# Perceiver block on one Trainium2 core: who turns the context of the first cross attention, and how it travels

## The chip, the cores and the metric

The kernel runs on one core of a Trainium2 chip. Its engines are TensorE (PE; PEld is its weight load), VectorE (DVE), ScalarE (ACT), GpSimd (POOL) and SyncE (SP), which here only issues DMA transfers. The metric is the device time of one execution in microseconds, as the median of several runs. Lower is better.

## The reference, cut to what matters

128 batches, each of 32 latents by 128 features (`x`) and 257 context rows by 128 features. Six residual stages follow each other; the change lies in the first, a cross attention with 16 heads of 64:

```python
xn = layer_norm(ctx_1024, g1, b1)                    # 257 rows a batch
ln_lat = layer_norm(layernorm(x), g2, b2)            # 32 rows a batch
q = ln_lat @ Wq
k, v = split(concatenate([xn, ln_lat], axis=1) @ Wkv)
weight = einsum('bhld,bhnd->bhln', q * scale, k * scale)   # 289 keys
weight = softmax(where(full_mask, weight, -max))
x = x + einsum('bhln,bhnd->bhld', weight, v) @ Wout
...
x = x + recurrence(x); x = x + ffn(x)
x = x + cross_attention_16_heads_of_8(x, ctx_1024)
x = x + self_attention(x); x = x + mixture_of_experts(x)
```

## The kernel before

The stages run one after another. The first cross attention is the function `xattn0`, and it is one software pipeline over the 128 batches: each engine runs `step(g, j)` for the step `s = 8g + j`, and within a step works on batches that are some steps ahead. `run_steps` writes the first 8 steps and those ahead of them out, loops over groups of 8, and writes the last ones out. Semaphores with growing counts order the engines; nothing else does, so the written order of each engine's `step` is the order of the work. The second cross attention (`xattn1`) uses `run_steps` too.

Weights are folded so that keys and values need no projection of their own. Scores of a batch are products of a query matrix (`qT`) and the transposed, normalised context (`xnT`, 256 columns of context, 32 of latents, one of the context's last row). Queries, and `xnT` too, are held as a rounded upper half (HI) and the rest (LO), and the score is a sum of three products. Four batches make a tile; once in four steps (`b == 0`) TensorE projects the finished tile (16 products, which the trace shows as `a_ctx<-U,a_oT` since they share a PSUM bank with the turned context).

One batch `n` passes as follows, by the step in which each thing happens before the change:

- `n-8`: SP loads its raw context (`load_raw`); `n-7`: VectorE takes mean and variance, GpSimd the reciprocal root; `n-6`: VectorE makes `z`, GpSimd multiplies by `g1` and adds `b1` (L671, L673), giving `xn`.
- `n-5`: TensorE turns the two halves of `xn` into the bank `a_ctx` (L884), between the two value products of another batch. ScalarE copies the bank to HI of `xnT` (L815), VectorE subtracts to get LO (L763).
- `n-3`: TensorE scores in four groups (L830), VectorE masks and takes the smallest (L705, "masks"), ScalarE takes the exponential with its sum (L778), VectorE the reciprocal (L755).
- `n-2`: ScalarE normalises the probabilities (L786, four instructions). VectorE transposes them in blocks of 32 x 32 into `blocks` (L716, 1024 columns; L718, 256 columns). `spread_prob` on SP then sends each of four quarters of `blocks` to `probT` (L625, four transfers of 192 KB), which completes the transposition. It waits for the blocks and for the value products that last read this one of the two `probT` buffers (`out_ready`).
- `n`: TensorE multiplies values and probabilities (L840, L847); ScalarE copies the result out in the next step (L796).

In every step TensorE also makes a quarter of the queries of a tile ahead (L856), ScalarE and VectorE split them (L811, L750). The order of VectorE's step is: masks, transposes, statistics, `z`, aggregation, query, reciprocal, (addition to `x`), LO of the context. That of ScalarE: result of the last batch, normalisation, four exponentials, query, HI of the context.

## Time and profile before

| | |
|---|---|
| median of 3 runs | 2055.96 us (2054.47 to 2059.8) |
| the profiled execution | 2053.8 us, of which its span 2051.7 us |
| granted TensorE clock, mean | 0.914 |
| PE busy | 1718.3 us, 84% |
| DVE busy | 1594.6 us, 78% |
| ACT busy | 1504.4 us, 73% |
| POOL busy | 908.9 us, 44% |
| DMA, all queues | 259.54 MB, mean 127 GB/s |

The span runs from the first to the last instruction of one profiled execution, and the time of that execution is a little longer. "Busy" is the time in which an engine's data path works; an engine's busy intervals can overlap with its next instruction's, so a group's busy sum can be less than count times duration. The clock is given as a share of full speed. Sizes such as 128x256 are partitions by elements.

### The profile page before, as it was taken

The numbers are of one execution on the slowest core, as the hardware profiler recorded it, in microseconds if no ns is written. First come the engines' busy times: TensorE is split into PE (matmuls) and PEld (weight loads), VectorE is DVE, ScalarE is ACT, GpSimd is POOL, SyncE is SP. The second block draws the span as 40 slices with busy tenths as digits, with TensorE's granted clock in tenths as the row PEclk, the third lists the DMA queues.
The fourth block names the chain that finished last, engine by engine and source line by source line (L and its number), as shares of the span: only waits on it lengthen the run. The fifth ranks groups of instructions, "written<-read, shape, count | busy, mean of one in ns | idle before, by whom it ended". The sixth has DMA issues, their size and how long they took to land. (4 is left out here: it accounts for less than half of the span.)

```text
span 2051.7 us, 51500 instructions
## 1 busy us (share of the span) xinstructions
PE 1718.3 (84%) x13455; PEld 1392.9 (68%) x13455; DVE 1594.6 (78%) x4998; ACT 1504.4 (73%) x4156; POOL 908.9 (44%) x1339
## 2 busy tenths in 40 slices
PE   3599999999999999971710679999999799749997
PEld 3489999999999999941500356666667566427775
DVE  4798888888888888837788669999999588636664
ACT  3488888888888888854765479999999588545553
POOL 1544444444444444304156034444444377335554
PEclk8599999999999999995755799999999799879998
DMA  4277676777777777610000059999999300103322
GB/s 139 85 167 165 160 160 157 161 163 162 159 162 163 159 160 164 151 42 0 0 0 0 2 147 250 252 250 251 249 249 248 73 1 0 32 13 102 91 87 82
DMA packets 196234, 259.54 MB, mean 127 GB/s; under 512 B 25136, under 2 KB 141328, under 8 KB 196032
## 3 DMA queue, kind: packets, MB, share of 16 engines
q1 hardware_dynamic: 194678, 256.53, 50.0%
q10 hardware_dynamic: 1194, 1.58, 0.3%
q0 software_dynamic: 288, 0.56, 0.1%
q8 instruction: 33, 0.54, 0.1%
q14 instruction: 41, 0.34, 0.0%
HBM read 86.09 MB, written 4.72 MB: 44 GB/s over the span
## 5 line engine op out<-in xcount | busy, mean ns | idle before, releaser
L778 ACT ACTIVATE a_prob<-a_neg,a_nmax 128x289 f32<-128x289 f32 x512 | 266.6, 525 | 1.4 <-DVE a_nmax L705 1.1
L840 PE MATMUL a_out<-a_probT,a_xn 128*128 128x256 f32 x1024 | 263.0, 380 | 5.0 <-DMA a_probT<-a_blocks 4.2
L1710 ACT ACTIVATE b_prob<-b_neg,b_nmax 128x257 f32<-128x257 f32 x512 | 260.6, 515 | 6.9 <-DVE b_nmax L1661 6.8
L671 POOL TENSOR_TENSOR a_xn<-a_z,g 128x256 f32<-128x256 f32 x128 | 93.8, 733 | 384.6 <-DVE a_z L739 384.6
L830 PE MATMUL a_score<-a_xnT,a_qT 128*128 128x290 f32 x1536 | 252.9, 314 | 2.5 <-DVE a_qT L750 2.5
L705 DVE CUSTOM_DVE_ANT_0 a_neg<-a_score,a_bias 128x289 f32<-128x289 f32 x512 | 211.6, 458 | 41.2 <-PE a_score L830 36.8
L786 ACT ACTIVATE a_prob<-a_prob,a_rinv 128x289 f32<-128x289 f32 x512 | 231.3, 527 | 1.8 <-DVE a_rinv L755 1.7
L830 PEld LDWEIGHTS a_score<-a_xnT,a_qT 128*128 128x128 f32 x1536 | 222.3, 190 | 9.6 <-issue 3.3
L1661 DVE CUSTOM_DVE_ANT_0 b_neg<-b_score,b_bias 128x257 f32<-128x257 f32 x512 | 188.6, 419 | 30.5 <-PE b_score L1801 15.3
L840 PEld LDWEIGHTS a_out<-a_probT,a_xn 128*128 128x128 f32 x1024 | 175.2, 191 | 19.8 <-DMA a_probT<-a_blocks 5.3
L716 DVE STREAM_TRANSPOSE a_blocks<-a_prob 128x1024 f32<-128x1024 f32 x128 | 159.4, 1245 | 24.0 <-ACT a_prob L786 17.7
L2417 POOL TENSOR_TENSOR m_hidden<-m_full,m_hidden 128x512 fp32r<-128x512 f32 (+1 forms) x88 | 113.7, 1292 | 106.6 <-ACT m_hidden L2398 106.6
L1672 DVE STREAM_TRANSPOSE b_blocks<-b_prob 128x1024 f32<-128x1024 f32 x128 | 156.3, 1221 | 0.2
L856 PE MATMUL a_q<-latT,A 128*128 (+1 forms) x1024 | 140.0, 281 | 12.4 <-DVE a_qT L750 10.1
L856 PEld LDWEIGHTS a_q<-latT,A 128*128 128x128 f32 x1024 | 131.0, 197 | 14.2 <-DVE a_qT L750 11.6
L847 PE MATMUL a_out<-a_probT,a_tail 128*128 128x256 f32 x512 | 131.4, 379 | 0.0
L796 ACT ACTIVATE a_oT<-a_out 128x512 f32<-128x512 f32 x128 | 76.6, 598 | 72.2 <-PE a_out L847 72.2
L872 PE MATMUL a_ctx<-U,a_oT 128*128 128x128 f32 x1024 | 119.7, 275 | 0.7 <-ACT a_oT L796 0.7
L2393 ACT ACTIVATE m_silu<-m_g 128x512 f32<-128x512 f32 (+1 forms) x88 | 52.7, 598 | 89.7 <-PE m_g L2047 89.7
L872 PEld LDWEIGHTS a_ctx<-U,a_oT 128*128 128x128 f32 x1024 | 116.9, 192 | 1.1 <-ACT a_oT L796 1.1
L1634 POOL TENSOR_TENSOR b_last_part<-b_v_rows,b_prob 128x128 f32<-128x128 f32 x128 | 52.0, 407 | 138.9 <-ACT b_prob L1710 134.1
L847 PEld LDWEIGHTS a_out<-a_probT,a_tail 128*128 128x128 f32 x512 | 97.3, 190 | 13.2
(478 smaller groups left out, 4567.9 us busy)
## 6 DMA issues: line engine op xcount, KB each, us to landing
a_probT<-a_blocks SPq DMA_DIRECT2D x512, 192.0 KB, 3.6
b_probT<-b_blocks SPq DMA_DIRECT2D x256, 256.0 KB, 4.6
a_raw<-in_ctx SPq DMA_DIRECT2D x128, 128.0 KB, 2.9
b_raw<-in_ctx SPq DMA_DIRECT2D x64, 256.0 KB, 4.7
m_wide<-expert_weights SPq DMA_DIRECT2D x128, 128.0 KB, 2.9
a_kept<-keep SPq DMA_DIRECT2D x32, 257.0 KB, 3.4
b_kept<-keep SPq DMA_DIRECT2D x32, 257.0 KB, 4.8
b_v_rows<-ctx_tail_values SPq DMA_DIRECT2D x32, 256.0 KB, 4.7
```

Of the source, the lines that this page charges most:

```text
L705: nc.vector.tensor_tensor_reduce(out=neg[:, grp, :], in0=score_ps[grp][:, 0:KEYS0], in1=bias[:, n, :], scale=-DH0 ** -0.5, scalar=3.4e38, ...
L716: nc.vector.transpose(blocks[:, n, :, 0:2].rearrange("p r t g l -> p g r t l"), prob[:, n, :, 0:2 * P].rearrange("p g (r t c) -> p g r t c ...
L778: nc.scalar.activation(prob[:, par, grp, 0:KEYS0], neg[:, grp, :], ACT.Exp, bias=nmax[:, par, grp:grp + 1], scale=-1.0, accum_out=rsum[:, ...
L786: last = nc.scalar.activation(part, part, ACT.Copy, scale=rinv[:, j % 2, grp:grp + 1])
L830: last = nc.tensor.matmul(score_ps[grp][:, 0:even(KEYS0)], qT[:, a, un, bn, 4 * grp:4 * grp + 4, :], xnT[:, c, n, :], start=(p == 0), stop ...
L840: nc.tensor.matmul(out_ps[:, half, 0:2 * P], xn[:, j, kt, :], probT[:, u, 2 * half:2 * half + 2, kt, :], start=(kt == 0), stop=False)
L847: last = nc.tensor.matmul(out_ps[:, half, 0:2 * P], tail[:, j, :], probT[:, j % 2, 2 * half:2 * half + 2, 2, :], start=False, stop=True)
L856: last = nc.tensor.matmul(q_ps[:, h * P:(h + 1) * P], k.A[:, 4 * hg + h, :], k.latT[:, ds((t + ahead) * P, P)], start=True, stop=True)
L872: last = nc.tensor.matmul(proj_ps, oT[:, slot, :], k.U[:, slot % GROUPS * HG + slot // GROUPS, :], start=(slot == 0), stop=(slot == H - 1))
L1661: nc.vector.tensor_tensor_reduce(out=neg[:, par, grp, :], in0=score_ps[grp][:, 0:N_CTX], in1=bias[:, n, :], scale=-DH1 ** -0.5, scalar=3.4 ...
L1672: nc.vector.transpose(blocks[:, n, :, j % 2].rearrange("p r t g l -> p g r t l"), prob[:, j % 4, :, 0:2 * P].rearrange("p g (r t c) -> p g ...
L1710: nc.scalar.activation(prob[:, (j + 5) % 4, grp, :], neg[:, par, grp, :], ACT.Exp, bias=nmax[:, par, grp:grp + 1], scale=-1.0, accum_out=r ...
```

## The change

- The context is no longer turned on TensorE. VectorE transposes `xn` in 32 x 32 blocks, in `turn_blocks`, into 64 more columns of `blocks`, six batches ahead; `spread_prob` carries them to `probT` together with the probabilities of the batch two ahead. Rows of both buffers grow from 384 to 448 elements, and each of the four transfers with them.
- HI of `xnT` is copied by ScalarE from the landed `probT` four batches ahead, behind the copy of the last result; LO is now subtracted by GpSimd, from SBUF. `spread_prob` waits also for that (`xnT_ready`), and VectorE's transposes of a buffer wait for its last landing.
- The bank `a_ctx` goes; the projection has its own, `a_proj`. `z` is written into `xn` directly.
- Raw context is loaded ten batches ahead instead of eight, its statistics taken eight ahead, `z` seven.
- VectorE's order becomes: statistics, masks, aggregation, transposes (context, then 256 columns, then 1024), `z`, (addition to `x`), query, reciprocal. ScalarE makes two exponentials ahead of the query and two behind. TensorE makes the first value products ahead of the query.
- The loops of `run_steps` begin at a block of the instruction fetch (`head_slot`), in both cross attentions; in the first the pipeline starts one step earlier and 16 batches instead of 8 are written out at the end.

The diff, without the parts that only move statistics, `z` and GpSimd's normalisation by a step:

```diff
-    with eng.Fori(1, (B - rest) // 8) as g:
+    with eng.bass.Fori(1, (B - rest) // 8, engines=[eng.engine], head_slot={eng.engine: 0}) as g:
...
-        blocks = sb("a_blocks", [P, 2, KEY_STEP, KEY_TILES, GROUPS, L])
-        probT = sb("a_probT", [P, 2, 4, KEY_TILES, P])
+        blocks = sb("a_blocks", [P, 2, KEY_STEP, KEY_TILES * P + 2 * L])
+        probT = sb("a_probT", [P, 2, 4, KEY_TILES * P + 2 * L])
...
-        ctx_ps, q_ps = psum("a_ctx"), psum("a_q")
-        proj_ps = ctx_ps[:, 2 * P:2 * P + D]
+        proj_bank, q_ps = psum("a_proj"), psum("a_q")
+        proj_ps = proj_bank[:, 0:D]
...
-        LEAD, LAG = 7, 1
+        LEAD, LAG, REST = 8, 1, 16
...
         def probT_loads(g, j):
...
-            return (g * 4 + (j // 2 + 1)) * 64
+            return (g * 4 + (j // 2 + 3)) * 64
...
+        def probs(n, kt, half):
...
+            return probT[:, n, 2 * half:2 * half + 2, kt * P:(kt + 1) * P]
...
+        def carried_ctx(j):
...
+            return probT[:, j % 2, :, KEY_TILES * P:].rearrange("p i (k m) -> p k i m", k=2 * KEY_STEP)
...
+        def ctx_cols(j, half):
...
+            return xnT[:, half, (j + 4) % 8, 0:2 * P].rearrange("p (k i m) -> p k i m", k=2 * KEY_STEP, i=4)
...
-                def load_raw(g, j):
-                    sp.dma_start(raw[:, j % 4], io["ctx_1024"][ds(g * 8 + j, 1), 0:2 * P, :].rearrange(
+                def load_raw(b, j):
+                    sp.dma_start(raw[:, j % 4], io["ctx_1024"][ds(b, 1), 0:2 * P, :].rearrange(
...
                 def spread_prob(g, j):
...
-                    wait_apart(k, sp, blocks_ready, s + 3)
+                    wait_apart(k, sp, blocks_ready, s + 7)
+                    if live(g, j, 4):
+                        wait_apart(k, sp, xnT_ready, s + 5)
...
-                        heads = slice(i * L, (i + 1) * L)
-                        sp.dma_start(probT[:, n, i].rearrange("p t q -> p (t q)"),
-                                     blocks[heads, n].rearrange("c r t g l -> c r (t g l)")).then_inc(probT_loaded[n], 16)
+                        sp.dma_start(probT[:, n, i], blocks[i * L:(i + 1) * L, n]).then_inc(probT_loaded[n], 16)
...
                 def step(g, j):
...
-                    if live(g, j, 8):
-                        if live(g, j, 4):
-                            wait_apart(k, sp, z_ready, s + 5)
-                        load_raw(g + 1, j)
+                    if live(g, j, 10):
+                        if live(g, j, 6):
+                            wait_apart(k, sp, z_ready, s + 7)
+                        load_raw(s + 10, j + 2)
...
-                    if live(g, j, 2):
+                    if live(g, j, 2) or live(g, j, 6):
...
+                    if live(g, j, 4):
+                        wait_apart(k, pool, xnT_hi, s + 5)
+                        nc.gpsimd.tensor_tensor(ctx_cols(j, LO), carried_ctx(j), ctx_cols(j, HI), ALU.subtract).then_inc(xnT_ready, 1)
...
-                    dve.wait_ge(prob_ready, s + 3)
-                    if live(g, j, 0):
+                    if live(g, j, 4) or live(g, j, 2):
...
-                    nc.vector.transpose(blocks[:, n, :, 0:2].rearrange("p r t g l -> p g r t l"),
-                                        prob[:, n, :, 0:2 * P].rearrange("p g (r t c) -> p g r t c", t=2, c=L))
-                    nc.vector.transpose(blocks[:, n, 0:2, 2].rearrange("p r g l -> p g r l"),
-                                        prob[:, n, :, 2 * P:2 * P + 2 * L].rearrange("p g (r c) -> p g r c", c=L)).then_inc(blocks_ready, 1)
+                    if live(g, j, 6):
+                        dve.wait_ge(xn_ready, s + 7)
+                        last = nc.vector.transpose(blocks[:, n, :, KEY_TILES * P:].rearrange("p f (r t m) -> p t f m r", r=KEY_STEP, t=2),
+                                                   xn[:, (j + 6) % 8].rearrange("p t (c f) -> p t f c", f=KEY_STEP))
+                    if live(g, j, 2):
+                        dve.wait_ge(prob_ready, s + 3)
+                        nc.vector.transpose(blocks[:, n, 0:2, 2 * P:3 * P].rearrange("p r (g l) -> p g r l", l=L),
+                                            prob[:, n, :, 2 * P:2 * P + 2 * L].rearrange("p g (r c) -> p g r c", c=L))
+                        last = nc.vector.transpose(blocks[:, n, :, 0:2 * P].rearrange("p r (t g l) -> p g r t l", t=2, l=L),
+                                                   prob[:, n, :, 0:2 * P].rearrange("p g (r t c) -> p g r t c", t=2, c=L))
+                    last.then_inc(blocks_ready, 1)
...
                 def step(g, j):
...
+                    if live(g, j, 2) or live(g, j, 6):
+                        turn_blocks(g, j)
+                    if live(g, j, 7):
+                        n, par = (j + 7) % 8, (j + 1) % 2
+                        wait(dve, out_ready, s)
+                        dve.wait_ge(rstd_ready, s + 8)
+                        for kt in range(2):
+                            last = nc.vector.tensor_scalar(xn[:, n, kt, :], raw[:, (j + 7) % 4, kt, :], mv[:, par, kt, 0:1],
+                                                           rstd[:, par, kt:kt + 1], ALU.subtract, ALU.mult)
+                        last.then_inc(z_ready, 1)
...
-                    if live(g, j, 5):
-                        dve.wait_ge(xnT_hi, s + 6)
-                        n = (j + 5) % 8
-                        nc.vector.tensor_tensor(xnT[:, LO, n, 0:2 * P], ctx_ps[:, 0:2 * P], xnT[:, HI, n, 0:2 * P],
-                                                ALU.subtract).then_inc(xnT_ready, 1)
...
+                def exps(g, j, groups):
...
+                    if live(g, j, 3):
+                        for grp in groups:
+                            exp(g, j, grp)
...
                 def step(g, j):
...
                     if live(g, j, -1):
...
+                    if live(g, j, 4):
+                        act.wait_ge(probT_loaded[j % 2], probT_loads(g, j))
+                        nc.scalar.activation(ctx_cols(j, HI), carried_ctx(j), ACT.Copy).then_inc(xnT_hi, 1)
                     if live(g, j, 2):
...
-                    if live(g, j, 3):
-                        for grp in range(GROUPS):
-                            exp(g, j, grp)
+                    exps(g, j, (0, 1))
...
-                    if live(g, j, 5):
-                        act.wait_ge(ctx_turned, s + 6)
-                        nc.scalar.activation(xnT[:, HI, (j + 5) % 8, 0:2 * P], ctx_ps[:, 0:2 * P], ACT.Copy).then_inc(xnT_hi, 1)
...
+                    exps(g, j, (2, 3))
...
-                        nc.tensor.matmul(out_ps[:, half, 0:2 * P], xn[:, j, kt, :], probT[:, u, 2 * half:2 * half + 2, kt, :],
+                        nc.tensor.matmul(out_ps[:, half, 0:2 * P], xn[:, j, kt, :], probs(u, kt, half),
...
                 def tail_values(g, j):
...
-                        last = nc.tensor.matmul(out_ps[:, half, 0:2 * P], tail[:, j, :], probT[:, j % 2, 2 * half:2 * half + 2, 2, :],
+                        last = nc.tensor.matmul(out_ps[:, half, 0:2 * P], tail[:, j, :], probs(j % 2, 2, half),
...
                         for grp in range(GROUPS):
...
+                    if here:
+                        values(g, j, 0)
...
-                        wait(pe, xnT_ready, s + 5 if live(g, j, 4) else B)
+                        wait(pe, x_added, t - 1)
...
-                        values(g, j, 0)
-                    if live(g, j, 5):
-                        n = (j + 5) % 8
-                        pe.wait_ge(xn_ready, s + 6)
-                        wait(pe, xnT_ready, s + 5)
-                        if b == 0:
-                            wait(pe, x_added, t)
-                        for kt in range(2):
-                            last = nc.tensor.transpose(key_order(ctx_ps[:, 0:2 * P], kt), xn[:, n, kt, :], k.ident[:])
-                        last.then_inc(ctx_turned, 1)
-                    if here:
```

TensorE in one ordinary step of the first cross attention (the third of a tile), behind the scores; before:

```order
L830 MATMUL a_score<-a_xnT,a_qT 128x290 [waits a_masked]
L830 MATMUL a_score<-a_xnT,a_qT 128x290 x2
L856 MATMUL a_q<-latT,A 128x128 [waits a_q_copied]
L856 MATMUL a_q<-latT,A 128x128 x3
L840 MATMUL a_out<-a_probT,a_xn 128x256 [waits a_oT_ready,a_probT_loaded0]
L840 MATMUL a_out<-a_probT,a_xn 128x256
L884 MATMUL a_ctx<-ident,a_xn 128x32x4 [waits a_xnT_ready,a_xn_ready]
L884 MATMUL a_ctx<-ident,a_xn 128x32x4
L840 MATMUL a_out<-a_probT,a_xn 128x256 x2
L847 MATMUL a_out<-a_probT,a_tail 128x256 x2
```

and with the change:

```order
L849 MATMUL a_score<-a_xnT,a_qT 128x290 [waits a_masked]
L849 MATMUL a_score<-a_xnT,a_qT 128x290 x2
L859 MATMUL a_out<-a_probT,a_xn 128x256 [waits a_oT_ready,a_probT_loaded0]
L859 MATMUL a_out<-a_probT,a_xn 128x256
L875 MATMUL a_q<-latT,A 128x128 [waits a_q_copied]
L875 MATMUL a_q<-latT,A 128x128 x3
L859 MATMUL a_out<-a_probT,a_xn 128x256 x2
L866 MATMUL a_out<-a_probT,a_tail 128x256 x2
```

The two turns are gone, and the wait for the landed probabilities stands ahead of the query products.

ScalarE in one step of the same stage, written out ahead of its loop; before:

```order
L796 ACTIVATE a_oT<-a_out 128x16x32 [waits a_out_ready]
L786 ACTIVATE a_prob<-a_prob,a_rinv 128x289 [waits a_rinv_ready]
L786 ACTIVATE a_prob<-a_prob,a_rinv 128x289 x3
L778 ACTIVATE a_prob,a_rsum<-a_neg,a_nmax 128x289 [waits a_masked] x4
L811 ACTIVATE a_qT<-a_q 128x4x4x32 [waits a_q_ready]
L815 ACTIVATE a_xnT<-a_ctx 128x256 [waits a_ctx_turned]
```

and with the change:

```order
L810 ACTIVATE a_oT<-a_out 128x16x32 [waits a_out_ready]
L825 ACTIVATE a_xnT<-a_probT 128x256 [waits a_probT_loaded1]
L800 ACTIVATE a_prob<-a_prob,a_rinv 128x289 [waits a_rinv_ready]
L800 ACTIVATE a_prob<-a_prob,a_rinv 128x289 x3
L792 ACTIVATE a_prob,a_rsum<-a_neg,a_nmax 128x289 [waits a_masked] x2
L832 ACTIVATE a_qT<-a_q 128x4x4x32 [waits a_q_ready]
L792 ACTIVATE a_prob,a_rsum<-a_neg,a_nmax 128x289 [waits a_masked] x2
```

The copy to `xnT` has moved from the step's end to its second place, and waits for a landing instead of for TensorE.

VectorE in one step, from the last mask to the end; before:

```order
L716 STREAM_TRANSPOSE a_blocks<-a_prob 128x4x4x2x32 [waits a_probT_loaded1,a_prob_ready]
L718 STREAM_TRANSPOSE a_blocks<-a_prob 128x4x2x32
L732 BN_STATS a_stats<-a_raw 128x6 [waits a_raw_loaded2]
L732 BN_STATS a_stats<-a_raw 128x6
L739 TENSOR_SCALAR a_z<-a_raw,a_mv,a_rstd 128x128 [waits a_xn_ready,a_rstd_ready]
L739 TENSOR_SCALAR a_z<-a_raw,a_mv,a_rstd 128x128
L746 BN_AGGR a_mv<-a_stats 128x2 [waits a_stats_ready]
L746 BN_AGGR a_mv<-a_stats 128x2
L750 TENSOR_TENSOR a_qT<-a_q,a_qT 128x4x4x32 [waits a_q_hi]
L755 RECIPROCAL a_rinv<-a_rsum 128x4 [waits a_exped]
L763 TENSOR_TENSOR a_xnT<-a_ctx,a_xnT 128x256 [waits a_xnT_hi]
```

and with the change:

```order
L755 BN_AGGR a_mv<-a_stats 128x2 [waits a_stats_ready]
L755 BN_AGGR a_mv<-a_stats 128x2
L730 STREAM_TRANSPOSE a_blocks<-a_xn 128x2x4x8x4 [waits a_xn_ready,a_probT_loaded0]
L734 STREAM_TRANSPOSE a_blocks<-a_prob 128x4x2x32 [waits a_prob_ready]
L736 STREAM_TRANSPOSE a_blocks<-a_prob 128x4x4x2x32
L764 TENSOR_SCALAR a_xn<-a_raw,a_mv,a_rstd 128x128 [waits a_rstd_ready,a_out_ready]
L764 TENSOR_SCALAR a_xn<-a_raw,a_mv,a_rstd 128x128
L773 TENSOR_TENSOR a_qT<-a_q,a_qT 128x4x4x32 [waits a_q_hi]
L778 RECIPROCAL a_rinv<-a_rsum 128x4 [waits a_exped]
L746 BN_STATS a_stats<-a_raw 128x6 [waits a_raw_loaded3]
L746 BN_STATS a_stats<-a_raw 128x6
```

Aggregation and the context's transpose stand ahead of those of the probabilities, and the subtraction at the end is gone.

## Rows read from the trace of the kernel before

**Rows 1.** Busy by stretch, four steps: stretch, length, engines' us (instructions), clock, DMA share, GB/s.
```profile
442.51:447.82 5.31, 5.31 (x36) 4.95 (x35) 5.20 (x22) 5.13 (x16) 4.63 (x11) 1.00 0.77 175
447.82:456.72 8.90, 8.90 (x69) 8.54 (x67) 6.81 (x25) 5.45 (x16) 4.68 (x8) 1.00 0.67 158
sum 24.84, PE 24.84 PEld 23.40 DVE 21.38 ACT 20.63 POOL 11.68; mean PE 6.21 PEld 5.85 DVE 5.34 ACT 5.16 POOL 2.92
```

**Rows 2.** Waits, 160 to 840 us: us in total, times, longest.
```profile
ACT a_xnT L815 <- PE a_ctx L884: 62.1, 27, 2.3
```

**Rows 3.** Timeline of PE through one ordinary step: start, length, instruction.
```profile
431.88 1.97 PE L830 MATMUL a_score<-a_xnT,a_qT 128*128 128x290 f32 x12
433.69 1.05 PE L856 MATMUL a_q<-latT,A 128*128 x8
...
435.44 0.38 PE L884 MATMUL a_ctx<-ident,a_xn 128*128 128x128 f32 x2
435.66 1.03 PE L840 MATMUL a_out<-a_probT,a_xn 128*128 128x256 f32 x4
```

**Rows 4.** Groups by form, 425.69 to 450.52 us: count, busy us, mean ns, idle before.
```profile
L716 DVE STREAM_TRANSPOSE a_blocks<-a_prob 128x1024 f32<-128x1024 f32 x4 | 5.0, 1246 | 0.7 <-ACT a_prob L786 0.5
...
L718 DVE STREAM_TRANSPOSE a_blocks<-a_prob 128x256 f32<-128x256 f32 x4 | 1.6, 402 | 0.0
L763 DVE TENSOR_TENSOR a_xnT<-a_ctx,a_xnT 128x256 fp32r<-128x256 f32 x4 | 1.6, 402 | 1.1 <-ACT a_xnT L815 1.1
L884 PE MATMUL a_ctx<-ident,a_xn 128*128 128x128 f32 x8 | 1.5, 273 | 0.0
```

**Rows 5.** Timeline of ACT in one step.
```profile
443.40 1.80 ACT L786 ACTIVATE a_prob<-a_prob,a_rinv 128x289 f32<-128x289 f32 x4
...
447.66 0.36 ACT L815 ACTIVATE a_xnT<-a_ctx 128x256 fp32r<-128x256 f32 x1
```

**Rows 6.** Queue in one step: timeline of SP; the last probability transfer alone, with its landing.
```profile
442.89 3.02 SPq L625 DMA_DIRECT2D a_probT<-a_blocks  x4
...
L625 SPq DMA_DIRECT2D a_probT<-a_blocks x1: 1001/1001/1001, 444.9 to 444.9; - x1
...
DMA to landing us min/median/max: 3.9/3.9/3.9
```

**Rows 7.** The same in the second cross attention (last two transfers).
```profile
1302.77 3.84 SPq L1583 DMA_DIRECT2D b_probT<-b_blocks  x4
...
L1583 SPq DMA_DIRECT2D b_probT<-b_blocks x2: 911/1180/1449, 1304.2 to 1305.2; - x2
...
DMA to landing us min/median/max: 4.9/5.0/5.1
```

**Rows 8.** The first spread of each attention: start, then its last transfers with their landing.
```profile
96.63 3.15 SPq L625 DMA_DIRECT2D a_probT<-a_blocks  x4
...
L625 SPq DMA_DIRECT2D a_probT<-a_blocks x2: 736/892/1049, 98.0 to 98.7; - x2
...
DMA to landing us min/median/max: 4.0/4.3/4.5
...
1208.98 3.88 SPq L1583 DMA_DIRECT2D b_probT<-b_blocks  x4
...
L1583 SPq DMA_DIRECT2D b_probT<-b_blocks x3: 601/1018/1562, 1209.6 to 1211.3; - x3
...
DMA to landing us min/median/max: 4.4/4.5/4.9
```

**Rows 9.** Timeline of DVE: the first mask of a step.
```profile
432.83 0.46 DVE L705 CUSTOM_DVE_ANT_0 a_neg<-a_score,a_bias 128x289 f32<-128x289 f32 x1 [1.24 <-PE a_score L830]
```

**Rows 10.** Fill of the pipeline (timeline) and waits in its drain (860 to 900 us).
```profile
78.61 0.72 POOL L673 TENSOR_TENSOR a_xn<-a_xn,b 128x256 f32<-128x256 f32 x1
...
86.69 3.24 PE L830 MATMUL a_score<-a_xnT,a_qT 128*128 128x290 f32 x12 [1.09 <-DVE a_qT L750]
...
PE a_out L840 <- DMA a_probT<-a_blocks: 4.2, 3, 2.1
```

78 lines of the change are left out of this document (33 added, 45 removed).

## The prediction

> **What bounds the kernel now.** I read the table by stage first, to see which engine never rests in the stretch that the change touches. Over four consecutive batches of the first cross attention TensorE is busy for all of 24.84 us, VectorE for 21.38, ScalarE for 20.63, GpSimd for 11.68 [rows 1]. One batch is one "step" below; three steps in four are ordinary (5.31 us) and the fourth, which also projects a finished tile, takes 8.90. The list of waits for 160 to 840 us then has no line of TensorE; it is led by ScalarE and GpSimd waiting for others, ScalarE for TensorE's turns [rows 2]. So this stage is bound by TensorE's own issue, and a TensorE instruction that goes saves its full spacing. But the slack of the others lies mostly in the projecting step: in the ordinary step shown ScalarE is busy for 5.13 of 5.31 and VectorE for 5.20 [rows 1].
>
> **What the change removes.** The two turns of the context lie between the value products: they begin at 435.44 and the next group at 435.66 [rows 3], so they hold TensorE for 0.22 us a step (their 273 ns each overlap with their neighbours [rows 4]). A step falls to 5.31 - 0.22 = 5.09 us, four steps to 24.84 - 0.88 = 23.96. Five of the 128 turns lie in the fill, where TensorE waits anyway, so some 122 steps save: -26.8 us. The reordering of value, query and projection products changes no TensorE work.
>
> **What it adds, and where.** VectorE loses the 256-column subtraction (402 ns) and gains a 256-column transpose, for which the one of the same size over the probabilities is the nearest row (402 ns) [rows 4]. Net nothing. Its source is strided, so it starts the next instruction after some 0.33, and I bound it from there to twice that; even 0.66 is covered, since VectorE then waits for the normalised probabilities (below). Without that cover it would cost 0.33 in each ordinary step, 30 us. GpSimd gains the subtraction; at 0.7 us, or even at 1.0, four of them on its 11.68 [rows 1] give 14.5 to 15.7 of 24, not a bound. Its result frees the carried buffer about 2 us into the step, long before the buffer can be sent again, and the scoring wants it a step later. ScalarE copies from SBUF instead of PSUM: between 0.36 (its length now) and 0.45 (a scaling of 289 columns from SBUF, 1.80/4) [rows 5]; I take 0.40. An ordinary ScalarE step becomes 5.12 + 0.04 = 5.16 against 5.09, a lag of 0.2 us over three steps that the projecting step gives back.
>
> The Trainium skill speaks against the exchange: VectorE: DVE Perf Modes, section Rules for kernel authors, sends a 128 x 128 transpose to TensorE where PSUM will do. By the rows that is the cheaper engine time (0.22 against 0.33), and if both engines were on the path the change would lose 0.11 a step, 14 us in all. Here only TensorE is on it, by rows 1 and 2, so I go by the rows.
>
> **The buffer's round trip** decides the rest. Each probability buffer now also carries the context, so ScalarE needs the landing at its second instruction of the step, not only TensorE at its value products, and the next sending needs normalisation and transposes that stand behind that copy. Let D be the time from the first of the four issues to the last landing. Now it is 442.89 to 444.9 + 3.9, so D = 5.9 [rows 6]. Each transfer grows from 192 to 224 KB. Bounds for the new D: the second cross attention sends 256 KB four times, from 1302.77 to 1305.2 + 5.1, D = 7.5 [rows 7]; halfway by size is 6.7. With little else moving, the first spreads of both stages take 98.7 + 4.5 - 96.63 = 6.6 and 1211.3 + 4.9 - 1208.98 = 7.2 [rows 8]; half of that difference gives 5.9 + 0.3 = 6.2. I take 6.35, nearer to the quiet pair because this stage's engines of the DMA still rest for a quarter of the time (share 0.77 [rows 1]), with 6.1 and 6.7 as ends and 6.9 for a queue that fills. The skill's DMA: Bandwidth & Descriptors, section Where 436 GB/s comes from, gives a ceiling of 435 GB/s; by it, as an estimate, 128 KB more would add 0.3 us and D would be 6.2.
>
> Now the longest path inside a group of four. Count from S, the end of the projecting step. Its buffer can be sent at S + 0.38 (TensorE's step at 442.51 against the issue at 442.89 [rows 1, 6]) and lands at S + 0.38 + D. Then: wake-up 0.10 (guess), copy 0.40, four normalisations 1.81, wake-up of VectorE 0.13, the two transposes of probabilities 0.33 + 1.25 [rows 4], wake-up of the queue 0.10: 4.12 us, then D again. The value products that need this second landing stand 1.81 us into the step (433.69 - 431.88 [rows 3]), three ordinary steps after S: 15.27 + 1.81 = 17.08. So the path is free while 0.38 + 4.12 + 2D is at most 17.08: D up to 6.29. Above it each group loses 2 x (D - 6.29). At 6.35 that is 0.12 us, times some 30 groups: +4 us.
>
> VectorE waits on that same path for the probabilities. Its masks begin 0.95 us into a step (432.83 against 431.88 [rows 3, 9]) or one own round after the last ones; with a round of 5.3 (5.20 busy [rows 1] and its small gaps) that is S + 6.25 in the second ordinary step, where the landing is late. Four masks take 1.7, aggregation and context transpose 0.5, so it is ready at S + 8.4; the probabilities are, by the path above, at S + 0.38 + 6.35 + 0.10 + 0.40 + 1.81 + 0.13 = 9.2. It then runs up to 1.4 us behind. The query product of the next step, now at 2.7 us into the step instead of 1.8, waits for VectorE's half of the query at about 1.8: covered.
>
> **Fill, drain, loops.** Before the first score the chain now has a transfer in it. Today that score begins at 86.69 behind the query chain [rows 10]; with the first context normalised at 79.3 [rows 10], transposed, and sent with D = 6 to 6.6, the first copy is at 86 to 87 and its subtraction a microsecond later, so the score moves 1 to 2 us, and each of the following sendings is a round trip of about 10 us, as now. I take +2 (0 to +5). In the drain TensorE already waits 4.2 us for these transfers [rows 10]; wider ones add about 1. Loading raw context two steps ahead moves one issue on the queue past the wait for the transposes, at no price: the issues end at 442.89 + 3.02 = 445.9 and the next step begins at 447.82 [rows 1, 6]. The loop heads: the back edges lie inside continuous work (TensorE is busy for all of each of these steps [rows 1]); I put them at 0, within 3 us either way, since the second cross attention's loops are moved too.
>
> Sum: -26.8 + 4 + 2 + 1 = -20 us. The profiled execution took 2053.8 us (span 2051.7), 2.2 below the median of the runs, so I forecast 2034 for it and **2036** as the median. A measurement tells this kernel from no change at about 0.3%, 6 us.
>
> **The rivals.**
> 1. The round trip eats the gain. For it: D near the halfway mark 6.7, which costs 0.8 a group, 24 us; and an ordinary step then keeps the DMA engines for 0.77 x 5.31 = 4.1 us, plus a sixth of the some 3.3 that are spreads, 4.6 of 5.09. Against: the queue of this stage rests a quarter of the time now. With D from 6.5 to 6.75 the time is 2045 to 2060, chance 0.17.
> 2. Slower: the wait for the landing takes TensorE's place as the bound, at the value products of the projecting step and the one before. It decides from D = 6.69, where 2 x (D - 6.29) x 30 exceeds the 24 left. At 6.9 the stage loses 37 us: 2053.8 - 24 + 37 and the 2.2 give about 2069. For it: D of the second attention, and raw loads issued right behind each spread. Chance 0.14.
> 3. The change does nothing: VectorE's strided transpose costs several times its row, say 1.2 us, so that VectorE needs 21.4 + 3.4 = 24.8 in four steps, as long as TensorE now. Nothing in the trace shows this layout. 2053 to 2060, chance 0.06.
> 4. All gain and no stall: D at 6.1 or less, 2031. It is the lower end of my forecast.
>
> **How the numbers follow.** The forecast with rival 4 (2029 to 2046) has 0.63. Faster by over 0.3% is that and a good third of rival 1: 0.70. Within 0.3%: the rest of rival 1 and half of rival 3: 0.13. Slower: rival 2 and what is left: 0.17. The range 2027 to 2061 leaves out most of rival 2 and a saving beyond the turns.
>
> **What would show it.** Right: no line for turns on TensorE; four steps of 23.96 to 24.2 us between the same instructions; D between 6.1 and 6.5; ScalarE's copy waiting on the landing by about 0.8 us in the third step of each group and nowhere else for long; GpSimd at about 60%; VectorE's idle time before the probability transposes growing. Wrong: long waits of TensorE's value products for the probability transfers over 160 to 840 us (rivals 1 and 2), a context transpose well over 0.4 us (rival 3), or four-step groups that stay at 24.8 though TensorE shows gaps.

## The result, and the profile after

The changed kernel takes **2073.5 us** (2071.6 to 2075.0, 4 runs) against 2056.5 for the kernel before in the same comparison: ratio 1.0082, interval 1.0069 to 1.0095. It is slower by 17 us; 2036 was forecast, and even the range (to 2061) was too low. The profiled execution took 2075.0 us, its span is 2073.2.

The profile says first where the time did not go. Table by stage of the changed kernel, four steps (columns as in [rows 1]):

```profile
440.17:445.26 5.09, 5.09 (x35) 4.78 (x33) 4.46 (x17) 4.71 (x14) 0.85 (x2) 1.00 0.65 130
445.26:450.75 5.49, 5.34 (x35) 4.81 (x33) 4.71 (x18) 4.41 (x13) 4.79 (x9) 1.00 0.86 213
450.75:456.01 5.26, 5.26 (x35) 4.82 (x33) 5.26 (x20) 5.26 (x17) 3.40 (x8) 1.00 0.81 182
456.01:464.96 8.95, 8.91 (x66) 8.37 (x65) 7.26 (x27) 6.22 (x20) 5.18 (x8) 1.00 0.73 188
sum 24.79, PE 24.61 PEld 22.78 DVE 21.68 ACT 20.59 POOL 14.22; mean PE 6.15 PEld 5.69 DVE 5.42 ACT 5.15 POOL 3.55
```

One step runs at exactly the forecast 5.09 us: the turns are gone and cost what was said. The next three are 0.40, 0.17 and 0.27 us too long, and 24.84 of before has become 24.79 instead of 23.96. Nearly all the gain inside the stage is eaten. The list of waits from 160 to 840 us shows by what:

```profile
ACT a_oT L810 <- PE a_out L866: 76.0, 28, 2.9
...
ACT a_xnT L825 <- DMA a_probT<-a_blocks: 40.4, 54, 1.7
...
DVE a_blocks L734 <- ACT a_prob L800: 22.4, 32, 1.4
PEld a_out L859 <- DMA a_probT<-a_blocks: 18.1, 52, 1.6
```

Before, TensorE stood in no line of this list. Now the weight loads of its value products (L859) wait for a landing 52 times, and ScalarE's copy (L825) 54 times. One group, read in order of time, is the forecast's path row by row. The queue, then the last transfers of its first sending with their landing, then ScalarE, VectorE, and TensorE:

```profile
440.55 3.62 SPq L637 DMA_DIRECT2D a_probT<-a_blocks  x4
...
451.23 3.60 SPq L637 DMA_DIRECT2D a_probT<-a_blocks  x4
```
```profile
L637 SPq DMA_DIRECT2D a_probT<-a_blocks x2: 933/1161/1389, 441.8 to 442.8; - x2
...
DMA to landing us min/median/max: 4.2/4.4/4.5
```
```profile
447.33 0.42 ACT L825 ACTIVATE a_xnT<-a_probT 128x256 fp32r<-128x256 f32 x1 [1.08 <-DMA a_probT<-a_blocks]
447.65 1.80 ACT L800 ACTIVATE a_prob<-a_prob,a_rinv 128x289 f32<-128x289 f32 x4
...
457.97 0.42 ACT L825 ACTIVATE a_xnT<-a_probT 128x256 fp32r<-128x256 f32 x1 [0.42 <-DMA a_probT<-a_blocks]
```
```profile
449.48 0.45 DVE L734 STREAM_TRANSPOSE a_blocks<-a_prob 128x256 f32<-128x256 f32 x1 [0.78 <-ACT a_prob L800]
449.85 1.20 DVE L736 STREAM_TRANSPOSE a_blocks<-a_prob 128x1024 f32<-128x1024 f32 x1
```
```profile
445.26 1.94 PE L849 MATMUL a_score<-a_xnT,a_qT 128*128 128x290 f32 x12
447.35 1.13 PE L859 MATMUL a_out<-a_probT,a_xn 128*128 128x256 f32 x4
...
456.01 1.95 PE L849 MATMUL a_score<-a_xnT,a_qT 128*128 128x290 f32 x12
457.99 1.13 PE L859 MATMUL a_out<-a_probT,a_xn 128*128 128x256 f32 x4
```

Sent at 440.55, landed at 442.8 + 4.5 = 447.3: D is 6.75 us, where it was 5.9 [rows 6]. Then copy, normalisation, transposes, the next sending at 451.23, which lands at 458.0, and TensorE begins its value products at 457.99. In this group the forecast's chain has no wrong link; its D has the wrong size.

The rest is outside the steady stretch. There are three pairs of rows, the changed kernel first and the kernel before second: start of the scores of the step that follows the first projecting one (fill), and of the last projecting step at a loop's end; then the last projection:

```profile
140.81 1.96 PE L849 MATMUL a_score<-a_xnT,a_qT 128*128 128x290 f32 x12
...
853.35 1.95 PE L849 MATMUL a_score<-a_xnT,a_qT 128*128 128x290 f32 x12
...
902.89 3.84 PE L893 MATMUL a_proj<-U,a_oT 128*128 128x128 f32 x32 [0.69 <-ACT a_oT L810]
```
```profile
133.61 1.96 PE L830 MATMUL a_score<-a_xnT,a_qT 128*128 128x290 f32 x12
...
845.53 1.97 PE L830 MATMUL a_score<-a_xnT,a_qT 128*128 128x290 f32 x12
...
890.15 3.84 PE L872 MATMUL a_ctx<-U,a_oT 128*128 128x128 f32 x32 [0.69 <-ACT a_oT L796]
```

In the fill of the changed kernel, the first score waits last for VectorE's half of a query; further on, a sending from 91.31 lands at 98.0, and the next one in its buffer starts at 101.93:

```profile
89.68 3.24 PE L849 MATMUL a_score<-a_xnT,a_qT 128*128 128x290 f32 x12 [1.51 <-DVE a_qT L773]
...
98.03 0.42 ACT L825 ACTIVATE a_xnT<-a_probT 128x256 fp32r<-128x256 f32 x1 [1.93 <-DMA a_probT<-a_blocks]
98.35 1.81 ACT L800 ACTIVATE a_prob<-a_prob,a_rinv 128x289 f32<-128x289 f32 x4
...
101.93 3.49 SPq L637 DMA_DIRECT2D a_probT<-a_blocks  x4
```

The fill is 7.2 us longer, the stretch between the two marks 0.6, the drain (from the second mark to the last projection) 49.54 - 44.62 = 4.9. The second cross attention, in which only the loop statement was changed, takes 448.5 us instead of 443.5 from its first to its last instruction. The routing stage behind it takes 2 us more and the other stages 1.8. Sum: 12.7 + 5.0 + 2.0 + 1.8 = 21.5, the difference of the spans.

### The profile page after: what moved, and what is told of

Its sections match the earlier page's. It is cut to its first block and busy times, and to the rows that moved or that the text cites. A ratio compares the mean times of both kernels' runs of the same rounds, so it can differ in the third digit from the quotient of the medians.

```text
span 2073.2 us, 51092 instructions
## 1 busy us (share of the span) xinstructions
PE 1718.7 (83%) x13199; PEld 1377.9 (66%) x13199; DVE 1606.9 (78%) x4998; ACT 1504.5 (73%) x4156; POOL 990.1 (48%) x1467
## 5 line engine op out<-in xcount | busy, mean ns | idle before, releaser
L859 PE MATMUL a_out<-a_probT,a_xn 128*128 128x256 f32 x1024 | 272.9, 390 | 19.1 <-DMA a_probT<-a_blocks 13.9
L718 DVE CUSTOM_DVE_ANT_0 a_neg<-a_score,a_bias 128x289 f32<-128x289 f32 x512 | 205.3, 454 | 21.9 <-PE a_score L849 17.2
L859 PEld LDWEIGHTS a_out<-a_probT,a_xn 128*128 128x128 f32 x1024 | 176.3, 191 | 52.4 <-DMA a_probT<-a_blocks 31.3
L702 POOL TENSOR_TENSOR a_xn<-a_xn,g 128x256 f32<-128x256 f32 x128 | 94.3, 737 | 220.5 <-DVE a_xn L764 220.5
L736 DVE STREAM_TRANSPOSE a_blocks<-a_prob 128x1024 f32<-128x1024 f32 x128 | 154.2, 1204 | 0.0
L875 PEld LDWEIGHTS a_q<-latT,A 128*128 128x128 f32 x1024 | 139.2, 198 | 21.1 <-DVE a_qT L773 12.0
L680 POOL TENSOR_TENSOR a_xnT<-a_probT,a_xnT 128x256 fp32r<-128x256 f32 x128 | 87.8, 686 | 78.8 <-ACT a_xnT L825 75.8
L893 PE MATMUL a_proj<-U,a_oT 128*128 128x128 f32 x1024 | 119.7, 275 | 0.7 <-ACT a_oT L810 0.7
L893 PEld LDWEIGHTS a_proj<-U,a_oT 128*128 128x128 f32 x1024 | 117.0, 192 | 1.1 <-ACT a_oT L810 1.1
```

Source lines behind the costliest of these rows:

```text
L718: nc.vector.tensor_tensor_reduce(out=neg[:, grp, :], in0=score_ps[grp][:, 0:KEYS0], in1=bias[:, n, :], scale=-DH0 ** -0.5, scalar=3.4e38, ...
L736: last = nc.vector.transpose(blocks[:, n, :, 0:2 * P].rearrange("p r (t g l) -> p g r t l", t=2, l=L), prob[:, n, :, 0:2 * P].rearrange("p ...
L859: nc.tensor.matmul(out_ps[:, half, 0:2 * P], xn[:, j, kt, :], probs(u, kt, half), start=(kt == 0), stop=False)
L875: last = nc.tensor.matmul(q_ps[:, h * P:(h + 1) * P], k.A[:, 4 * hg + h, :], k.latT[:, ds((t + ahead) * P, P)], start=True, stop=True)
L893: last = nc.tensor.matmul(proj_ps, oT[:, slot, :], k.U[:, slot % GROUPS * HG + slot // GROUPS, :], start=(slot == 0), stop=(slot == H - 1))
```

## The experiments

"Changed" is the kernel with the change; each ratio is to the kernel before, from runs of the same comparison. "Group" is the mean of sixteen groups of four steps in the profiled execution, measured between the starts of projection products in the middle of the stage, D the mean over some 70 sendings there, from the first issue to the last landing. A profiled execution can differ from its kernel's median: it took 2050.6 with the values late (median 2053.9), 2063.5 with the new heads in the first only (2068.7), 2034.4 with four edits (2038.2).

| kernel | median us | ratio, interval | group us | D us |
|---|---|---|---|---|
| before | 2056 | 1 | 24.86 | 5.99 |
| changed | 2073.5 | 1.0082 (1.0069, 1.0095) | 24.74 | 6.61 |
| sends 384 columns | 2045.5 | 0.9951 (0.9939, 0.9963) | 23.97 | 6.01 |
| sends 512 columns | 2127.3 | 1.0345 (1.0331, 1.0359) | 26.32 | 7.44 |
| before, sends 448 | 2057.6 | 1.0009 (1.0000, 1.0018) | 24.86 | 6.64 |
| values late | 2053.9 | 0.9986 (0.9975, 0.9997) | 24.24 | 6.62 |
| copy late | 2064.4 | 1.0053 (1.0039, 1.0067) | 24.60 | - |
| short ends | 2067.9 | 1.0055 (1.0042, 1.0068) | 24.75 | - |
| four edits | 2038.2 | 0.9915 (0.9902, 0.9929) | 23.93 | 6.58 |
| and query first | 2034.9 | 0.9893 (0.9878, 0.9908) | 24.04 | - |
| plain loops | 2113.3 | 1.0278 (1.0264, 1.0291) | 26.60 | - |
| new heads in the first only | 2068.7 | 1.0061 (1.0047, 1.0075) | 24.73 | - |
| before, new heads | 2066.1 | 1.0053 (1.0039, 1.0067) | 24.86 | - |

### Is it the landing? A dose in both directions

```diff
-                        sp.dma_start(probT[:, n, i], blocks[i * L:(i + 1) * L, n]).then_inc(probT_loaded[n], 16)
+                        sp.dma_start(probT[:, n, i, 0:KEY_TILES * P],
+                                     blocks[i * L:(i + 1) * L, n, :, 0:KEY_TILES * P]).then_inc(probT_loaded[n], 16)
...
+                nc.gpsimd.memset(probT[:, :, :, KEY_TILES * P:], 0.0)
```

> The changed kernel sending only the 384 columns of the probabilities; the 64 columns of the context are not sent, so all scores over the context are made from zeros (this part of the computation is wrong, all instructions of the engines stay). Theory A: the landing is what holds a group of four steps at 24.8 us; with D back from 6.75 to 5.9-6.1 us a group takes 24.0 us and the run 2073.5 - 0.8 x 30 - some 3 of fill and drain = 2044 to 2049. Theory B: VectorE, whose turns of the context take 0.65 us, or ScalarE holds it: groups stay at 24.6 or more and the run above 2065.

2045.5 us, group 23.97. Every engine runs the instructions of the changed kernel, on a context of zeros, and the whole forecast gain of the groups is there. TensorE is busy again for all of the sixteen groups, first row below; the second is the kernel of the other direction, which sends 64 idle columns more:

```profile
328.35:711.86 383.51, 383.51 (x2563) 363.56 (x2562) 348.20 (x1249) 328.98 (x961) 227.53 (x417) 1.00 0.73 167
```
```profile
351.35:772.50 421.15, 394.56 (x2563) 364.98 (x2561) 350.24 (x1248) 330.38 (x961) 227.20 (x416) 1.00 0.81 192
```

```diff
-        blocks = sb("a_blocks", [P, 2, KEY_STEP, KEY_TILES * P + 2 * L])
-        probT = sb("a_probT", [P, 2, 4, KEY_TILES * P + 2 * L])
+        blocks = sb("a_blocks", [P, 2, KEY_STEP, KEY_TILES * P + 4 * L])
+        probT = sb("a_probT", [P, 2, 4, KEY_TILES * P + 4 * L])
...
```

The cut part keeps the readers and the writer of the context to the first 64 of the 128 columns behind the probabilities.

> The changed kernel sending 512 columns, 64 of them zeros that nobody reads: 256 KB a step instead of 224. By the forecast's formula a group of four loses 2 x (D - 6.29). With D grown by as much as from 384 to 448 columns, from 6.75 to 7.5 or 7.6, a group takes 24.8 + 1.6 = 26.3 to 26.5 us and the run 2073.5 + 28 x 1.6 = 2115 to 2122. If the landing is not what holds the groups, it stays below 2085.

2127.3 us, group 26.32: within the expected 26.3 to 26.5; the run is 5 us beyond, in fill and drain (each some 3 us longer than in the changed kernel). Above 23.96 the groups lose 0.78 us at D = 6.61 and 2.36 at 7.44; the formula 2 x (D - 6.29) gives 0.64 and 2.30. The threshold and the slope of the forecast hold, to 0.1 us a group.

The converse, the same width where nothing early waits for it:

```diff
-        blocks = sb("a_blocks", [P, 2, KEY_STEP, KEY_TILES, GROUPS, L])
-        probT = sb("a_probT", [P, 2, 4, KEY_TILES, P])
+        sent = sb("a_blocks", [P, 2, KEY_STEP, KEY_TILES * P + 2 * L])
...
+        landed = sb("a_probT", [P, 2, 4, KEY_TILES * P + 2 * L])
...
-                        heads = slice(i * L, (i + 1) * L)
-                        sp.dma_start(probT[:, n, i].rearrange("p t q -> p (t q)"),
-                                     blocks[heads, n].rearrange("c r t g l -> c r (t g l)")).then_inc(probT_loaded[n], 16)
+                        sp.dma_start(landed[:, n, i], sent[i * L:(i + 1) * L, n]).then_inc(probT_loaded[n], 16)
```

> The kernel before with the width of the changed transfers and nothing else: it sends 448 columns instead of 384, of which the last 64 are zeros that nobody reads. Theory A (a longer landing costs only where something early in the step waits for it; here the first reader is the value products at 2.7 us): groups stay at 24.8, fill and drain grow by 1 to 3 us: 2056 to 2060. Theory B (the wider transfers cost by themselves, by the port or the queue): 2065 or more.

2057.6 us, group 24.86 to the second decimal, at D = 6.64. A slower landing by itself costs this stage nothing in the steps; its last projection comes 22.1 us after the one before it instead of 19.7, so the drain pays some 2.4 us for width. The medians differ by 1.4 us.

### Giving the path room again

```diff
                     if live(g, j, 3):
                         for grp in range(GROUPS):
                             score(g, j, grp)
-                    if here:
-                        values(g, j, 0)
...
                     if here:
+                        values(g, j, 0)
                         values(g, j, 1)
```

> The changed kernel with the first value products of a step back behind the query and projection products, as the kernel before had them; nothing else. In an ordinary step they then need their landing 0.9 us later (2.7 instead of 1.8 us into the step), and the path inside a group is free up to D = 6.74 us, against 6.75 measured. Theory A (landings wait at the first value products): groups of 24.0 to 24.2 us, 2073.5 - 0.7 x 30 = 2050 to 2054, and no more waits of TensorE for these transfers in the steady stretch. Theory B (VectorE or ScalarE holds the group): within 4 us of 2073.

2053.9 us, and no line of TensorE waiting for these transfers from 300 to 700 us. The first value products ahead of the query took 0.9 us of slack from the landing, and that one reordering costs 20 us. Groups are 24.24, not 23.96, though D (6.62) is under the 6.74 that the forecast's formula then allows, so the formula leaves out 0.28 us a group. ScalarE's copy still waited 33 times in those 400 us, 23.6 us in all, and VectorE's transposes behind it 17 times for the probabilities, 12.1 us. TensorE shows no idle time, but in the group from 326.67 its query products begin 1.93 and 1.91 us after the scores in the third ordinary step and in the projecting one, against 1.80 in the first two. The third:

```profile
342.83 1.96 PE L849 MATMUL a_score<-a_xnT,a_qT 128*128 128x290 f32 x12
344.76 1.16 PE L875 MATMUL a_q<-latT,A 128*128 x8
```

With ScalarE's copy moved as well (below, Together) the groups are at 23.93, so the copy's place holds this rest; that it does so by VectorE's half of the query is argued from these rows. The other cut of the path, ScalarE's copy behind the normalisation, alone:

```diff
+                    if live(g, j, 2):
+                        normalise(g, j)
                     if live(g, j, 4):
                         act.wait_ge(probT_loaded[j % 2], probT_loads(g, j))
                         nc.scalar.activation(ctx_cols(j, HI), carried_ctx(j), ACT.Copy).then_inc(xnT_hi, 1)
-                    if live(g, j, 2):
-                        normalise(g, j)
```

> The changed kernel with ScalarE's copy of the landed context put behind the normalisation instead of ahead of it; nothing else. The forecast's path (landing, copy, normalisation, transposes, next sending) is then cut, but a second one is as long in this kernel: landing, the values of that step with the query between them (3.3 us), the next sending. Theory A (the two paths are about equal, so cutting one gives nothing inside the groups): groups stay at 24.7 to 24.8 us, fill shorter by 1 to 2 us since the first normalisation no longer waits for a landing: 2069 to 2073. Theory B (the copy's place is the whole of it): groups of 24.2, 2056 to 2060.

2064.4, groups 24.60: neither theory's number. The groups give 0.14 (some 4 us), the first projection comes 3.3 us sooner, more than expected. TensorE's value products still wait for the landing, their weight loads 28 times from 300 to 700 us, 8.4 us in all. So the second path (landing, values, next sending) is nearly as long, as theory A says, but not quite.

### The ends

```diff
+                    cols = slice(0 if live(g, j, 2) else KEY_TILES * P, KEY_TILES * P + 2 * L if live(g, j, 6) else KEY_TILES * P)
                     for i in range(4):
-                        sp.dma_start(probT[:, n, i], blocks[i * L:(i + 1) * L, n]).then_inc(probT_loaded[n], 16)
+                        sp.dma_start(probT[:, n, i, cols], blocks[i * L:(i + 1) * L, n, :, cols]).then_inc(probT_loaded[n], 16)
```

> The changed kernel sending only what is used at the two ends: the 64 context columns in the first four sendings, the 384 of the probabilities in the last six. The fill was 7.2 us longer than before and the drain 4.9. Theory A (the width of the transfers makes them longer): first landings 1.5 to 3 us sooner, drain shorter by 2 to 3, together 2073.5 - 4 to - 7 = 2066 to 2069. Theory B (it is the number of round trips in a row and their fixed part): 2071 to 2074.

2067.9: theory A. A first sending lands after 3.9 us instead of 7.1; the first projection comes 2.4 us sooner, and the last three projections lie 2.2 us closer together. The first projection alone is a weak sign: where only the second attention's loop heads differ (next section) it came 1.3 us sooner too.

### The loop heads

```diff
-    with eng.bass.Fori(1, (B - rest) // 8, engines=[eng.engine], head_slot={eng.engine: 0}) as g:
+    with eng.Fori(1, (B - rest) // 8) as g:
```

> The changed kernel with the loop statement of the kernel before (no fetch-block head), all else as changed. The second cross attention took 443.5 us before and 448.5 after, though the change touches nothing in it but its loops. Theory A: the loop heads cost this, and the stage falls back by 5 us: 2073.5 - 5 = 2068 to 2069 us, 2066 if the routing stage gives back its 2 us too. Theory B: the stage is longer because all its code and buffers stand elsewhere now: no change, 2072 to 2075.

2113.3 us: 40 us slower, which neither theory held possible. The second cross attention does fall back, to 444.4 us; the routing stage does not give back its 2 us but takes 58.1. And the first grows by 39: the timeline of VectorE shows one stall at each back edge:

```profile
365.50 0.16 DVE L778 RECIPROCAL a_rinv<-a_rsum 128x4 f32<-128x4 f32 x1
369.86 0.29 DVE L746 BATCH_NORM_STATS2 a_stats<-a_raw 128x6 f32<-128x128 f32 x1 [4.20 <-issue]
```

Waits, 160 to 840 us, the same stall and what stands behind it:

```profile
DVE a_stats L746 <- issue: 47.2, 12, 4.2
...
PE a_score L849 <- DVE a_qT L773: 30.2, 12, 3.0
```

Twelve stalls, one a pass, 47.2 us in all; "issue" means that the engine waited for nothing that the profile shows. TensorE then waits twelve times for VectorE's half of the query. In the changed kernel as given, the first line has 1.6 us in all and the second is missing. The Trainium skill (Runtime: NRT & Kernel Launch, section Instruction fetch mechanics) says that a taken branch to code outside what is held forces a fetch before the engine goes on; the trace agrees in that a stall of 4 us stands at a loop's start and waits for nothing. That the 4 us are such a fetch is not shown by itself: the kernel before has the plain loop and no such stall, with 275 instructions of VectorE in the trace of one pass against 279. Whether the place of the code makes the difference was not tried.

The same edit the other way round, on the kernel before:

> The kernel before with only the loop heads of the change. Theory A (the heads cost the second cross attention 5 us): 2056.5 + 5 = 2061 to 2063 us. Theory B (its position in the code does): 2055 to 2058, or a shift of either sign of up to 5 us that the first theory does not give.

2066.1 us: 10 slower, more than theory A gave. The groups of the first cross attention are unchanged (24.86) but for the two at its way into the loop, which are 1.7 us longer together. The second grows from 443.5 to 452.6, most of it on its first way into the loop, where TensorE stands still once for no visible wait:

```profile
1248.03 1.24 PE L1764 MATMUL b_score<-b_kT,b_qbd 32*128 32x257 f32 x8 [6.45 <-issue]
```

The heads in the first attention alone:

```diff
-    with eng.bass.Fori(1, (B - rest) // 8, engines=[eng.engine], head_slot={eng.engine: 0}) as g:
+    loop = eng.bass.Fori(1, (B - rest) // 8, engines=[eng.engine], head_slot={eng.engine: 0}) if heads \
+        else eng.Fori(1, (B - rest) // 8)
...
```

> The changed kernel with the new loop heads in the first cross attention alone; the second has the old loop statement. Theory A: the 4 us at 1257 us, where the queue of SP enters its loop, and what follows go; the second cross attention falls from 448.5 to 444 to 446 us, the run to 2069 to 2071. Theory B (it is the place of the code, not the heads): 2072 to 2076.

2068.7 us, 5 less than the changed kernel. The second cross attention is back at 443.6. The routing takes 54.2 instead of 56.3, but that is no sign of the heads: over all the kernels it takes 54.2 to 58.1, and the 58.1 stand in the changed kernel with plain loops. Queue of SP where it enters the second attention's loop, changed kernel, then this one:

```profile
1254.08 4.46 SPq L1593 DMA_DIRECT2D b_probT<-b_blocks  x4
1263.16 0.42 SPq L1577 DMA_DIRECT2D b_raw<-in_ctx  x1
```
```profile
1250.43 3.66 SPq L1595 DMA_DIRECT2D b_probT<-b_blocks  x4
1254.46 0.40 SPq L1579 DMA_DIRECT2D b_raw<-in_ctx  x1
```

With the new head the queue stands still from 1258.5 to 1263.2, once; without it, 0.4 us. All seven versions of the changed kernel with a head there have this stop once, of 4.0 to 4.6 us, and none of the four with the plain loop there has it. The length of the whole stage varies by more than that: 445.4 to 450.1 us in the seven, 443.6 to 447.2 in the four. So the stop is the head's; what the stage pays for it is less sure: 5 us in this pair, 2.7 between the means of the seven and the four.

### What VectorE's turn costs

```diff
-                        last = nc.vector.transpose(blocks[:, n, :, KEY_TILES * P:].rearrange("p f (r t m) -> p t f m r", r=KEY_STEP, t=2),
-                                                   xn[:, (j + 6) % 8].rearrange("p t (c f) -> p t f c", f=KEY_STEP))
+                        nc.vector.transpose(blocks[:, n, 2:4, 2 * P:2 * P + 2 * L],
+                                            xn[:, (j + 6) % 8, 0].rearrange("p (c f) -> p f c", f=KEY_STEP))
+                        last = nc.vector.transpose(blocks[:, n, :, KEY_TILES * P:].rearrange("p f (r t m) -> p t f m r", r=KEY_STEP, t=2)[:, 1],
+                                                   xn[:, (j + 6) % 8, 1].rearrange("p (f c) -> p f c", f=KEY_STEP))
```

> A measurement of VectorE's turn of the context (652 ns against 402 ns for the same 256 columns of probabilities): it is split into two turns of 128 columns, one with only its source strided (4 elements apart), written contiguously, one with only its destination strided and its source contiguous. The context that arrives is therefore wrong. If the strided source costs it, the first is near 0.35 us or more and the second near 0.2 to 0.25; if the scattered destination does, the other way about; if it is the number of dimensions of the pattern, both lie near 0.3. The time: up to 0.2 us more VectorE work a step, hidden or not, 2073 to 2082.

Groups by form, 300 to 700 us: the strided source (L730), the scattered destination (L732), and the probabilities' 256 columns (L736).

```profile
L736 DVE STREAM_TRANSPOSE a_blocks<-a_prob 128x256 f32<-128x256 f32 x65 | 27.2, 419 | 14.1 <-ACT a_prob L802 13.6
...
L730 DVE STREAM_TRANSPOSE a_blocks<-a_xn 128x128 f32<-128x128 f32 x65 | 24.9, 384 | 0.0
L732 DVE STREAM_TRANSPOSE a_blocks<-a_xn 128x128 f32<-128x128 f32 x65 | 23.2, 357 | 0.0
```

Either one alone takes nearly as long for 128 columns as the compact form for 256, so neither side alone is to blame; that both lie somewhat above the 0.3 us of the third case leaves open what the number of dimensions adds. The run took 2071.3 us, one time only, so the split costs nothing that this could show.

### Together

Four of the diffs above on the changed kernel: values late, copy late, short ends, and the new heads in the first cross attention alone.

> Four edits together on the changed kernel: first value products behind query and projection (2053.9 by itself), ScalarE's copy behind the normalisation, short sendings at both ends, and the loop heads at a fetch block only in the first cross attention. If the parts add: 2053.5 - 4 (heads of the second attention) - 4 (ends) - 2 (fill by the copy's place) = 2041 to 2046 us, with groups of 23.96 to 24.05. If the groups are already free in the run with late values, the copy's place gives nothing there; if VectorE or ScalarE becomes the bound, groups stay above 24.1.

2038.2 us, 18 less than before, 35 less than the change and 3 to 8 less than the parts add up to; the groups are at 23.93 and TensorE never rests in them. Sixteen groups:

```profile
322.81:705.75 382.94, 382.94 (x2563) 363.12 (x2561) 345.26 (x1249) 330.01 (x961) 228.98 (x417) 1.00 0.80 189
```

One more edit on top (`query_low` is VectorE's half of a query, as it was, made a function):

```diff
...
+                    if isinstance(g, int) and s < -2:
+                        query_low(g, j)
                     if live(g, j, 2) or live(g, j, 6):
                         turn_blocks(g, j)
...
+                    if not (isinstance(g, int) and s < -2):
+                        query_low(g, j)
```

> The version of four edits, with one more: in the fill (steps -8 to -3) VectorE makes its half of a query ahead of the turn and the normalisation of a context, instead of behind them. Theory A: what is left of the longer fill is the chain of the four query products, which now waits for VectorE's normalisations (the first score begins at 90.8 us there, and its context has been there since 87): the first score comes 2 to 3 us sooner and the run falls from 2038 to 2035 or 2036. Theory B: the fill is set by the contexts' round trips (the second and third score wait for GpSimd's subtraction behind a landing): within 1 us of 2038.

2034.9 us. The first score begins at 88.76 instead of 90.83; 0.9 of that is a setup that ended earlier in this execution, so the order gives 1.2 us there. That the run gains by it is not shown: the intervals of the two versions overlap, and of the two profiled executions this one is the longer (2036.7 against 2034.4), with groups of 24.04 though nothing in the loop was changed. Either version beats both kernels.

## Why the prediction was wrong

- **Removed work: right.** Steps of 5.09 us appear (440.17 to 445.26), and where no reader waits for the landing a group takes 23.93 to 23.97 against the forecast 23.96 (384 columns sent, and four edits; 24.04 with the fifth).
- **The path inside a group: right in form, wrong in one term, and this is the step that failed.** The term is D = 6.35 "nearer to the quiet pair". It measured 6.75 in the group shown, just beyond the end of 6.7, and 6.61 in the mean. The reasoning was that queue load adds little here; but sending the same width in the kernel before gives 6.64, and 512 columns 7.44. So each 32 KB more a transfer adds 0.6 to 0.8 us, and the point halfway by size, 6.7, was the better estimate. With D = 6.61 to 6.75 the forecast's own formula 2 x (D - 6.29) gives 0.64 to 0.92 us a group where it took 0.12; 0.78 was lost. The groups in the middle lose 0.65 more than said; three behind the fill and at the loop's end are 4.7 us longer still, for a cause that was not separated. Together 23.4 of the 41.5 us between the forecast span and the measured one.
- **Rival 1 is what happened in the steps.** Its price, up to 2060, fits the first attention's steady stretch. It was given 0.17 because the DMA share left room. The share was no measure of the round trip: between the changed kernel (0.78 over sixteen groups) and the one that sends 512 columns (0.81) it hardly moves, and D goes from 6.61 to 7.44. Rival 2's 2069 lies nearer to the result, by luck: its sign is a stage slower than before, and the groups are still 0.12 us shorter than before; the run is slower by fill, drain and what lies behind the stage.
- **Fill: +2 taken, +7.2 measured.** The first score moved 3.0 us and not 1 to 2, and it waits last for VectorE's half of a query, which the forecast left where it was, though the change put it behind the context's transpose and `z`. Then each of the first sendings waited for the landing of the last one in the same buffer, and for the copy and the normalisation behind it. Narrow sendings give back 2.4 at the first projection, the copy's place 3.3, and the order of query and normalisation on VectorE 1.2 in the version of four edits, each read in one trace. The fill is 5.2 us of the error.
- **Drain: +1 taken, +4.9 measured,** half of it width; 3.9 us of the error.
- **Loop heads: "0, within 3" was the wrong question.** They hide 40 us in the first attention that its new code would otherwise lose, and cost 3 to 5 in the second. The second attention is 5.0 us of the error; the routing's 2.0 and the other stages' 1.8 have no cause shown. The forecast looked at back edges that cost nothing in the kernel before, and took them to stay so.
- **VectorE's turn** took 652 ns, the upper end, and the cover held, as argued: with 384 columns sent no line of the waits names it.
- **What was moved:** the reordering "changes no TensorE work", true, and costs 20 us: it sets the 1.81 in the forecast's own formula. Had the values stayed at 2.7 us into the step, the threshold would have been 6.74. (With the values put back there, 0.28 us a group was still lost.) The text had both numbers, and the sum used D's best guess, 0.06 us over the threshold, without asking what 0.3 us more would cost.

The Trainium skill's ceiling of 435 GB/s (DMA: Bandwidth & Descriptors, section Where 436 GB/s comes from) had given D = 6.2 as an estimate; the measured 6.6 speaks against using it there: 4 x 32 KB more in 0.62 us is some 210 GB/s, half of it.

## What to carry to other kernels

Where a path is free up to a threshold and costs twice its excess beyond, compare the estimate's error with the distance to the threshold: here D was 0.3 to 0.4 us over its estimate, and some 19 us went in the middle of the stage. When data ride along with a transfer, list their first readers: each one that stands earlier in its engine's step takes slack from the sender. Test a loop head by itself in every loop it is put on; the same statement saved 40 us in one and cost 3 to 5 in another.

## What the runs showed of the hardware

- A back edge of VectorE's loop of eight steps can cost 4 us each time (twelve times, 47.2 us in all), or nothing, for nearly the same code; with the head at a fetch block the same line waits 1.6 us in all. Entering the second attention's loop with such a head stops SP's queue once, for 4.0 to 4.6 us in seven kernels, or TensorE once for 6.45 us in the kernel before.
- The four transfers of one sending land, from first issue, after 6.0, 6.6 and 7.4 us for 192, 224 and 256 KB each, whichever of the kernels sends them (5.99 and 6.01 for 192 KB, 6.61 and 6.64 for 224).
- A transpose of 32 x 32 blocks of f32 on VectorE runs at about half speed when either side is strided: 384 and 357 ns for 128 columns, 652 for 256 with both, against 402 to 419 for 256 compact ones. As an estimate from the compact rows (256 columns in 402 ns, 1024 in 1200 to 1246), a compact column takes 1.0 to 1.1 ns and the instruction some 130 ns besides; the strided ones then take 1.8 to 2.0 ns a column.
